# Second attention: where the queries' sums are added, and when the query parts, the one-hot products and the exponentials are issued

## The chip, the cores and the metric

The kernel runs on one core of one Trainium2 chip. The metric is the device time of one execution in microseconds, as the median over runs; lower is better. The profile of one further execution lists, for the same core, the busy time of every engine, the waits and the granted clock of TensorE.

## What is computed

The program is two layers, each a cross attention and a mixture of experts, on x of 4 x 256 x 512 in float32, with a context of 4 x 1601 x 512. The change lies in the second layer's attention alone:

```
def _L1_xattn_ref(text, features, Wq_w, Wq_b, Wk_w, Wk_b, fn_w, qn_w, kn_w):
    def rmsnorm(x, w):
        xf = x.astype(jnp.float32)
        var = jnp.mean(xf * xf, axis=-1, keepdims=True)
        return (xf * jax.lax.rsqrt(var + EPS)).astype(x.dtype) * w
    features_n = rmsnorm(features, fn_w)
    Q = jnp.einsum('btd,fd->btf', text, Wq_w) + Wq_b
    K = jnp.einsum('bsd,fd->bsf', features_n, Wk_w) + Wk_b
    Q = rmsnorm(Q, qn_w)
    K = rmsnorm(K, kn_w)
    scale = 1.0 / jnp.sqrt(jnp.asarray(K.shape[-1], dtype=Q.dtype))
    scores = jnp.einsum('btf,bsf->bts', Q, K) * scale
    attn = jax.nn.softmax(scores, axis=-1)
    attended = jnp.einsum('bts,bsf->btf', attn, features_n)
    return attended
x = x + _L1_xattn_ref(_layernorm(x, axis=-1), ctx_4096, ...)
```

## The kernel before

**Numbers in two parts.** Every large product is made of float32 operands split into a high part (rounded to the fast matmul format, made by ScalarE as a copy) and a low part (value minus high part, made by VectorE or GpSimd). TensorE then runs three matmuls for one product: high by high, high by low, low by high (the helper `three`, L1580 to L1582).

**Query part** (engine programs of `normed_attention_block`, before the loops). The 1024 rows of x are 8 tiles of 128; a batch i of 4 has two of them. For each batch TensorE transposes x (`transpose_x`, L1618), multiplies by the query weights in four column groups f (`project`, 12 matmuls of 256 columns each, into two halves of `ps_s` in turn), and one batch later multiplies the queries by the scaled key weights (`through_keys`, 4 x 12 matmuls). This way the keys are never projected: the scores are the queries, taken through the key weights, times the normalised context. ScalarE makes the high part of the queries (`qt_hi`, L1862) and their squares (L1864); VectorE makes the low part (`qt_lo`, L2012). `project` of group f waits for `qt_done` of group f - 2, since they share a half of `ps_s`. What the RMS norm of Q and the key bias need per query row are two sums over 512 features: of the squares, and of the query times `z_col` (norm weights times key bias). `query_sums` (L1643 to L1662) makes them as matmuls of one column in plain float32: per tile 4 for the squares (L1655), and 8 for the other sum (L1658 and L1660). The trace shows each plain float32 matmul as two instructions.

**Loop.** One iteration is one batch b, with 13 tiles of 128 context rows (the last has 65).

- Tile steps: ScalarE scales a tile (`scale_tile`), TensorE transposes it (L1668), ScalarE and VectorE split it into `k_hi` and `k_lo` (L1830, L1966), TensorE multiplies it by the Gram matrix of the key weights (`key_products`), VectorE adds a row (L2034) and sums it against the tile (L2036, two operands in SBUF) to get the norm of each key. ScalarE and GpSimd split the tile itself into `f_hi` and `f_lo` (L1895, L1566). At t = 1 ScalarE also writes `q_hi` of the batch (L1897), and at t = 2 GpSimd writes `q_lo` (L1574).
- Key norms: they lie one per partition and are needed along the columns. `turn_norms` transposes them, ScalarE takes the root, VectorE inverts (`invert`, L2047), and `spread_inverses` (L1723) multiplies with a one-hot matrix, so that every partition holds the row. These matmuls have 8 or 5 rows. ScalarE copies the result (`key_inverses`, L1884).
- Scores: `scores(j, ch)` for two query tiles j and four column chunks ch. VectorE scales them and takes the maximum (`scale_scores`, `largest`), ScalarE takes the exponential in two halves (`exponents`, L1910).
- Weighing: in eight steps (j, g) TensorE transposes the weights (`transpose_probs`, L1763), ScalarE and VectorE split them (`probs_hi` L1924, `probs_lo` L2069), and `weigh` multiplies by the context tiles. `output` (L2076 on) adds the result to x.

Each engine runs its own list in the order in which it is written, with semaphore waits between the engines; nothing reorders it. In the list of TensorE before, the lines that matter here stand so:

```
                    key_products(t)
                    if t == FIRST + 1:
                        turn_norms(0)
                spread_inverses(0)
...
                scores(0, 1)
                scores(0, 0).then_inc(s_ps, 1)
                scores(0, 2)
                turn_norms(1)
                scores(0, 3).then_inc(s_ps, 1)
                spread_inverses(1)
```

## Time and profile before

| What | Value |
|---|---|
| median of 3 runs | 3189.24 us (3187.05 to 3197.71) |
| profiled execution, its own time | 3184.14 us |
| its span, first to last instruction | 3182.4 us |
| TensorE matmul busy (PE) | 3049.8 us, 96% of the span |
| VectorE busy (DVE) | 2046.9 us, 64% |
| ScalarE busy (ACT) | 1727.0 us, 54% |
| GpSimd busy (POOL) | 871.5 us, 27% |
| mean granted clock of TensorE | 0.979 of full speed |

PE counts a matmul as busy from start to a modelled end, so it is also busy when it runs at half clock. "PEclk" in a table of stretches is the granted clock as a share of full speed (1 is 2.4 GHz, 0.5 is 1.2 GHz), averaged over the stretch; so stretch x (1 - PEclk) is the time that the lower clock cost in it, as long as TensorE had work. A row of the timeline gives start, length, engine, line, operation, and in brackets the idle time before it and what ended it.

### The profile page before, as it was taken

How to read it: one execution, taken by the hardware profiler on the slowest of the kernel's cores; microseconds unless marked ns; L12 is line 12 of the kernel's file. 1: busy time of each engine (PE TensorE's matmuls, PEld its weight loads, DVE VectorE, ACT ScalarE, POOL GpSimd, SP SyncE). 2: the span in 40 equal slices, each digit the busy share in tenths (PEclk: the TensorE clock that was granted, in tenths of full speed). 3: DMA queues.
4: the chain of work that ended last, by engine and by line, in shares of the span. 5: the costliest groups of instructions: out<-in, count | busy, mean ns of one | idle time of the engine just before them, and what ended most of it. 6: DMA issues, size and time to landing. Idle time of an engine off the chain costs nothing. (4 is left out here: it accounts for less than half of the span.)

```text
span 3182.4 us, 53416 instructions
## 1 busy us (share of the span) xinstructions
PE 3049.8 (96%) x18474; PEld 2704.4 (85%) x18474; DVE 2046.9 (64%) x3205; ACT 1727.0 (54%) x3218; POOL 871.5 (27%) x709
## 2 busy tenths in 40 slices
PE   8999998999999999999999999979979899998898
PEld 8888887899999999899998999978858897776786
DVE  4433333788888888788887888864464546554676
ACT  4433344667766666666666666642243334443473
POOL 0000121344444444444443444432200122221202
PEclk9999999999999999999999999999989989999999
DMA  7665696767777676677766777557631110111685
GB/s 251 217 215 197 206 289 201 151 159 163 163 159 163 159 159 161 155 158 158 162 159 156 158 161 161 129 143 240 203 133 77 34 36 29 41 41 40 213 290 163
DMA packets 376184, 497.59 MB, mean 156 GB/s; under 512 B 34348, under 2 KB 283484, under 8 KB 375928
## 3 DMA queue, kind: packets, MB, share of 16 engines
q1 hardware_dynamic: 373368, 485.93, 56.5%
q0 software_dynamic: 2560, 8.39, 0.8%
q8 instruction: 143, 2.34, 0.3%
q14 instruction: 113, 0.93, 0.1%
HBM read 226.09 MB, written 133.87 MB: 113 GB/s over the span
## 5 line engine op out<-in xcount | busy, mean ns | idle before, releaser
L725 POOL TENSOR_TENSOR a_t_lo<-a_turned,a_t_hi 128x512 fp32r<-128x512 f32 x512 | 649.7, 1290 | 938.5 <-ACT a_t_hi L854 938.5
L845 ACT ACTIVATE a_probs<-a_ps_s,a_neg_max 128x1024 f32<-128x1024 f32 (+1 forms) x512 | 529.5, 1034 | 474.4 <-DVE a_neg_max L897 468.7
L890 DVE TENSOR_REDUCE a_half_max<-a_ps_s 128x1 f32<-128x1024 f32 (+1 forms) x512 | 571.2, 1116 | 190.9 <-PE a_ps_s L742 186.8
L740 PE MATMUL a_ps_s<-a_k_buf,a_q_buf 128*128 128x512 f32 (+1 forms) x1024 | 419.6, 410 | 17.8 <-ACT a_probs L845 11.7
L741 PE MATMUL a_ps_s<-a_k_buf,a_q_buf 128*128 128x512 f32 (+1 forms) x1024 | 386.0, 377 | 0.0
L742 PE MATMUL a_ps_s<-a_k_buf,a_q_buf 128*128 128x512 f32 (+1 forms) x1024 | 385.1, 376 | 0.0
L926 DVE TENSOR_TENSOR a_x_lo<-a_ps_x,a_x_hi 128x512 fp32r<-128x512 f32 (+1 forms) x512 | 314.4, 614 | 107.1 <-ACT a_x_hi L863 107.1
L916 DVE STREAM_TRANSPOSE a_turned<-xn 128x512 f32<-128x512 f32 x512 | 357.7, 699 | 0.0
L472 DVE TENSOR_TENSOR p_out<-p_ps_j,p_out 128x512 fp32r<-128x512 f32 (+3 forms) x196 | 152.9, 780 | 303.8 <-ACT p_out L400 303.8
L400 ACT ACTIVATE p_out<-p_ps_j 128x512 fp32r<-128x512 f32 (+3 forms) x196 | 142.1, 725 | 312.0 <-PE p_ps_j L293 312.0
L740 PE MATMUL a_ps_o<-a_t_hi,a_v_buf 128*128 128x256 f32 x1024 | 298.9, 292 | 6.1 <-issue 3.6
L854 ACT ACTIVATE a_t_hi<-a_turned 128x512 fp32r<-128x512 f32 x512 | 298.5, 629 | 2.3 <-DVE a_turned L916 2.3
L863 ACT ACTIVATE a_x_hi<-a_ps_x 128x512 fp32r<-128x512 f32 (+1 forms) x512 | 274.5, 537 | 24.5 <-PE a_ps_x L770 12.8
L741 PE MATMUL a_ps_o<-a_t_lo,a_v_buf 128*128 128x256 f32 x1024 | 287.5, 281 | 0.0
L742 PE MATMUL a_ps_o<-a_t_hi,a_v_buf 128*128 128x256 f32 x1024 | 287.3, 281 | 0.0
L770 PE MATMUL a_ps_x<-a_turn,a_probs 128*128 128x128 f32 (+1 forms) x1792 | 279.1, 272 | 0.0
L740 PE MATMUL a_ps_o<-a_x_hi,a_v_buf 128*128 128x256 f32 (+1 forms) x896 | 262.4, 293 | 0.0
L742 PE MATMUL a_ps_o<-a_x_hi,a_v_buf 128*128 128x256 f32 (+1 forms) x896 | 251.8, 281 | 0.0
L741 PE MATMUL a_ps_o<-a_x_lo,a_v_buf 128*128 128x256 f32 (+1 forms) x896 | 251.4, 281 | 0.0
L770 PEld LDWEIGHTS a_ps_x<-a_turn,a_probs 128*128 128x128 f32 (+1 forms) x1792 | 219.0, 140 | 34.8 <-issue 0.2
L740 PEld LDWEIGHTS a_ps_s<-a_k_buf,a_q_buf 128*128 128x128 f32 x1024 | 194.9, 190 | 48.6 <-issue 11.7
L742 PEld LDWEIGHTS a_ps_s<-a_k_buf,a_q_buf 128*128 128x128 f32 x1024 | 194.6, 190 | 34.3
(437 smaller groups left out, 6944.6 us busy)
## 6 DMA issues: line engine op xcount, KB each, us to landing
xn<-a_probs SPq DMA_DIRECT2D x1024, 128.0 KB, 3.4
a_q_all<-p_out SPq DMA_DIRECT2D x64, 512.0 KB
a_q_buf<-a_q_all SPq DMA_DIRECT2D x128, 256.0 KB, 3.1
a_k_buf<-a_k_all SPq DMA_DIRECT2D x64, 464.5 KB, 4.0
a_v_all<-p_out SPq DMA_DIRECT2D x56, 512.0 KB
a_k_all<-p_out SPq DMA_DIRECT2D x48, 384.0 KB
a_v_buf<-a_v_all SPq DMA_DIRECT2D x64, 256.0 KB
a_o_all<-a_o_part SPq DMA_DIRECT2D x128, 128.0 KB, 3.1
```

The lines of the kernel that those rows point to most:

```text
L472: dve.tensor_tensor(job_views(n, 1)[0], ps, hi.bitcast(F32), ALU.subtract).then_inc(job_done, 1)
L725: pool.tensor_tensor(t_lo[:, slot, :, :], turned[:, slot, :, :], t_hi[:, slot, :, :].bitcast(F32), ALU.subtract).then_inc(t_done, 1)
L740: pe.matmul(o, w_hi, m_hi, start=first, stop=False)
L741: pe.matmul(o, w_hi, m_lo, start=False, stop=False)
L742: return pe.matmul(o, w_lo, m_hi, start=False, stop=last)
L770: tr = pe.transpose(ps_x[0:rows, bank, col:col + P], probs[j][u.a][:, c0:c0 + rows], turn[:, :])
L845: act.activation(probs[j][u.a][:, lo:hi], s_flat[:, lo:hi], ACT.Exp, bias=neg_max[:, j:j + 1], scale=SCALE, accum_out=half_sum[:, bass.ds( ...
L854: act.activation(t_hi[:, slot, :, :], turned[:, slot, :, :], ACT.Copy).then_inc(t_hi_done, 1)
L863: act.activation(x_hi[0:rows, slot, 0:m, :], ps_x[0:rows, bank, 0:TOK * m].rearrange("p (m n) -> p m n", m=m), ACT.Copy).then_inc(x_hi_don ...
L890: dve.reduce_max(half_max[:, half:half + 1], s_flat[:, lo:hi], AX.X).then_inc(max_done, 1)
L916: dve.transpose(turned[:, slot, :, :].rearrange("p k (q r) -> p k q r", r=SQ), traded[:, u.a, :, :, 2 * SQ * p:2 * SQ * (p + 1)].rearrange ...
L926: dve.tensor_tensor(x_lo[0:rows, slot, 0:m, :], ps_x[0:rows, bank, 0:TOK * m].rearrange("p (m n) -> p m n", m=m), x_hi[0:rows, slot, 0:m, ...
```

## The change

1. `query_sums` no longer sums over the four feature groups on TensorE. ScalarE writes a third tile per group, `biased_q` = (query + bias) x `z_col` (with a new column `z_bias`). GpSimd adds the four groups of the squares and of `biased_q` to one, each with an addition of 2 x 256 columns and one of 256, and TensorE makes one matmul of one column per sum and tile. VectorE's `qt_lo` now waits for the third tile (`q_read`) instead of the second.
2. The split of the scaled key weights (`w2_hi`, `w2_lo`) moves from the first batch of queries to a place ahead of the split of the query weights.
3. `q_hi` and `q_lo` of a batch are made during the weighing of the batch before (ahead of the loop for the first one), and `q_lo` by VectorE instead of GpSimd.
4. `spread_inverses(0)` moves behind `scores(0, 0)`.
5. The two exponentials of the second query tile move ahead of `probs_hi(0, 2)` and `probs_hi(0, 3)`.

```diff
@@ gpsimd
             pool.memset(k_lo[:, :, CTX:WIDTH].bitcast(F32), 0.0).then_inc(set_up, 1)
+            for i in range(B):
+                pool.wait_ge(q_read, DC * (i + 1))
+                for n, parts in enumerate((squared[i % 2], biased_q[i % 2])):
+                    pool.tensor_tensor(parts[:, 0:2, :], parts[:, 0:2, :], parts[:, 2:4, :], ALU.add).then_inc(q_added, 1)
+                    pool.wait_ge(q_added, 4 * i + 2 * n + 1)
+                    pool.tensor_tensor(parts[:, 0, :], parts[:, 0, :], parts[:, 1, :], ALU.add).then_inc(q_added, 1)
             pool.wait_ge(table_done, 3)
...
-                    if t == 2:
-                        pool.wait_ge(q_hi_done, b + 1)
-                        pool.tensor_tensor(q_lo[:, :, :].rearrange("p c n -> p (c n)"), queries[:, bass.ds(b, 1), :].rearrange("p a n -> p (a n)"),
-                                           q_hi[:, :, :].rearrange("p c n -> p (c n)").bitcast(F32), ALU.subtract).then_inc(q_done, 1)
@@ tensor
             def query_sums(i):
-                pe.wait_ge(q_squared, DC * (i + 1))
+                pe.wait_ge(q_added, 4 * (i + 1))
...
                 for j in range(QT):
                     at = QT * i + j
-                    for f in range(DC):
-                        pe.matmul(ps_p[:, 0, at:at + 1], squared[i % 2][:, f, j * P:(j + 1) * P], ones[:, 0:1],
-                                  start=f == 0, stop=f == DC - 1)
-                    for f in range(DC):
-                        pe.matmul(ps_p[:, 1, at:at + 1], qt_hi[i % 2][:, f, j * P:(j + 1) * P].bitcast(F32), z_col[:, f:f + 1],
-                                  start=f == 0, stop=False)
-                        mm = pe.matmul(ps_p[:, 1, at:at + 1], qt_lo[i % 2][:, f, j * P:(j + 1) * P].bitcast(F32), z_col[:, f:f + 1],
-                                       start=False, stop=f == DC - 1)
+                    pe.matmul(ps_p[:, 0, at:at + 1], squared[i % 2][:, 0, j * P:(j + 1) * P], ones[:, 0:1], start=True, stop=True)
+                    mm = pe.matmul(ps_p[:, 1, at:at + 1], biased_q[i % 2][:, 0, j * P:(j + 1) * P], ones[:, 0:1], start=True, stop=True)
                 mm.then_inc(qs_ps, 1)
...
-                spread_inverses(0)
...
                 scores(0, 0).then_inc(s_ps, 1)
+                spread_inverses(0)
                 scores(0, 2)
@@ scalar
                 normalize(t)
+            act.wait_ge(qk_w_done, 1)
+            for f in range(DC):
+                act.activation(w2_hi[:, f, :], key_w[:, f, :], ACT.Copy, scale=qk_w[:, f:f + 1]).then_inc(w2_hi_done, 1)
             weights_hi(0)
...
-                if i == 0:
-                    for f in range(DC):
-                        act.activation(w2_hi[:, f, :], key_w[:, f, :], ACT.Copy, scale=qk_w[:, f:f + 1]).then_inc(w2_hi_done, 1)
...
+                    act.activation(biased_q[i % 2][:, f, :], ps_s[:, f % 2, 0:TOK], ACT.Identity, scale=z_col[:, f:f + 1], bias=z_bias[:, f:f + 1]
+                                   ).then_inc(q_read, 1)
...
+            act.wait_ge(q_kept, DC)
+            query_hi(0)
             with act.Fori(0, B) as b:
...
-                    if t == 1:
-                        act.activation(q_hi[:, :, :].rearrange("p c n -> p (c n)"), queries[:, bass.ds(b, 1), :].rearrange("p a n -> p (a n)"),
-                                       ACT.Copy).then_inc(q_hi_done, 1)
...
-                exponents(0)
+                exponents(0, 0)
+                exponents(0, 1)
                 probs_hi(0, 0)
                 probs_hi(0, 1)
                 scale_tile(b + 1, 0)
                 scale_tile(b + 1, 1)
+                exponents(1, 0)
                 probs_hi(0, 2)
+                exponents(1, 1)
                 probs_hi(0, 3)
-                exponents(1)
 
                 act.activation(table_seed[:, :], eps_col[:, :], ACT.Sqrt)
+                query_hi((b + 1) % B)
@@ vector
+            dve.tensor_tensor(z_bias[:, :], z_col[:, :], columns[:, BQ, :], ALU.mult).then_inc(z_done, 1)
+            for f in range(DC):
+                dve.wait_ge(w2_hi_done, f + 1)
+                dve.scalar_tensor_tensor(w2_lo[:, f, :], key_w[:, f, :], qk_w[:, f:f + 1], w2_hi[:, f, :].bitcast(F32),
+                                         ALU.mult, ALU.subtract).then_inc(w2_done, 1)
             weights_lo(0)
...
-                    dve.wait_ge(q_squared, DC * i + f + 1)
+                    dve.wait_ge(q_read, DC * i + f + 1)
...
+            query_lo(0, 1)
             with dve.Fori(0, B) as b:
...
                 probs_lo(1, 1)
+                query_lo((b + 1) % B, b + 2)
                 output(0)
```

**Sums of a batch, on TensorE.** The end of `through_keys(0)` (L1582) and the start of `query_sums(0)`, before; the pair of `z_col` rows stands four times per tile, and the whole twice:

```order
L1582 MATMUL c_ps_s<-c_k_hi,c_f_lo 128x256
L1655 MATMUL c_ps_p<-ones,c_shared 128x1 x4
L1658 MATMUL c_ps_p<-c_z_col,c_k_hi 128x1
L1660 MATMUL c_ps_p<-c_z_col,c_k_lo 128x1
L1658 MATMUL c_ps_p<-c_z_col,c_k_hi 128x1
```

The same place in the change, with the transposes of x and the next product behind it (the names in `c_shared` are the added squares and the added `biased_q`; line numbers are those of the changed kernel):

```order
L1585 MATMUL c_ps_s<-c_k_hi,c_f_lo 128x256
L1656 MATMUL c_ps_p<-ones,c_shared 128x1
L1657 MATMUL c_ps_p<-ones,c_shared 128x1
L1656 MATMUL c_ps_p<-ones,c_shared 128x1
L1657 MATMUL c_ps_p<-ones,c_shared 128x1
L1621 MATMUL c_ps_t<-ident,xn 128x128 x8
L1583 MATMUL c_ps_s<-c_k_hi,c_f_hi 128x256
```

Of 24 matmuls of one column per batch 4 are left.

**One-hot products, on TensorE.** The end of the last key product, `spread_inverses(0)` and the start of the scores, before:

```order
L1581 MATMUL c_ps_s<-c_g_lo,c_k_hi 65x128
L1582 MATMUL c_ps_s<-c_g_hi,c_k_lo 65x128
L1723 MATMUL c_ps_p<-c_key_row,key_w 128x128 x8
L1778 REGISTER_ALU
L1580 MATMUL c_ps_s<-c_k_hi,c_q_hi 128x512
```

The same products in the change, between the last matmuls of `scores(0, 0)` and the first of `scores(0, 2)`:

```order
L1583 MATMUL c_ps_s<-c_k_hi,c_q_hi 128x512
L1584 MATMUL c_ps_s<-c_k_lo,c_q_hi 128x512
L1585 MATMUL c_ps_s<-c_k_hi,c_q_lo 128x512
L1719 MATMUL c_ps_p<-c_key_row,key_w 128x128 x8
L1583 MATMUL c_ps_s<-c_k_hi,c_q_hi 128x512
```

They moved behind 24 matmuls of 512 columns.

**Exponentials, on ScalarE.** From the scaling of the next batch's second tile (`c_raw`) to the switch back to the table of the root, before:

```order
L1824 ACTIVATE c_raw<-c_raw,c_inverse 128x512
L1917 REGISTER_ALU
L1923 ISA
L1924 ACTIVATE c_t_hi<-c_ps_t 128x512
L1917 REGISTER_ALU
L1923 REGISTER_ALU
L1924 ACTIVATE c_t_hi<-c_ps_t 65x128
L1910 ACTIVATE c_shared,c_half_sum<-c_shared,c_neg_max,c_q_now 128x1024
L1910 ACTIVATE c_shared,c_half_sum<-c_shared,c_neg_max,c_q_now 128x577
L1936 ACT_TABLE_LOAD
```

And in the change:

```order
L1820 ACTIVATE c_raw<-c_raw,c_inverse 128x512
L1912 ACTIVATE c_shared,c_half_sum<-c_shared,c_neg_max,c_q_now 128x1024
L1919 REGISTER_ALU
L1925 ISA
L1926 ACTIVATE c_t_hi<-c_ps_t 128x512
L1912 ACTIVATE c_shared,c_half_sum<-c_shared,c_neg_max,c_q_now 128x577
L1919 REGISTER_ALU
L1925 REGISTER_ALU
L1926 ACTIVATE c_t_hi<-c_ps_t 65x128
L1940 ACT_TABLE_LOAD
```

Each half of the second tile's exponential now stands ahead of one of the two copies `c_t_hi` that it followed.

## Rows read from the trace of the kernel before

**Rows 1.** Busy time by stretch: queries, then the four iterations; count, PEclk, DMA share, GB/s.

```profile
2501.00:2585.30 84.30, 82.36 (x599) 81.59 (x598) 22.22 (x45) 20.26 (x44) 0.00 (x0) 0.85 0.01 3
2585.30:2669.70 84.40, 80.55 (x437) 68.95 (x438) 45.59 (x82) 36.88 (x66) 20.80 (x15) 0.93 0.13 40
2669.70:2754.40 84.70, 78.81 (x437) 66.87 (x436) 49.01 (x82) 36.73 (x66) 20.27 (x15) 0.96 0.13 39
2754.40:2837.60 83.20, 77.29 (x438) 65.64 (x437) 48.99 (x82) 36.80 (x66) 20.33 (x15) 0.98 0.11 39
2837.60:2922.40 84.80, 78.89 (x437) 66.61 (x435) 49.02 (x82) 36.77 (x66) 20.34 (x15) 0.96 0.13 39
```

**Rows 2.** Waits of PE, 2501 to 2922 us: total, times, longest.

```profile
PE c_ps_s L1580 <- DVE c_k_lo L1966: 7.6, 13, 1.4
PE c_ps_t L1763 <- ACT c_shared L1910: 6.6, 4, 1.7
PE c_ps_p L1723 <- DVE c_key_row L2047: 6.3, 8, 1.4
PE c_ps_s L1580 <- DVE c_k_lo L2012: 1.9, 2, 1.6
```

**Rows 3.** Busy time by stretch: first and last `query_sums`, and what follows.

```profile
2521.60:2528.10 6.50, 6.50 (x51) 6.50 (x49) 0.42 (x1) 0.00 (x0) 0.00 (x0) 0.81 0.00 0
...
2577.60:2585.30 7.70, 7.70 (x50) 7.70 (x49) 0.42 (x1) 0.00 (x0) 0.00 (x0) 0.67 0.00 0
2585.30:2590.30 5.00, 5.00 (x21) 4.71 (x22) 1.75 (x6) 2.65 (x5) 1.44 (x2) 0.50 0.00 0
```

**Rows 4.** Timeline of PE: start and slowing of the first `query_sums`.

```profile
2521.61 0.95 PE L1655 MATMUL c_ps_p<-ones,c_shared 128*128 128x1 f32 x8
...
2525.54 0.54 PE L1658 MATMUL c_ps_p<-c_z_col,c_k_hi 128*128 128x1 f32 x2
```

**Rows 5.** Timeline: a query group in the third batch, from ScalarE to TensorE's next-but-one group.

```profile
2532.60 0.48 ACT L1862 ACTIVATE c_k_hi<-c_ps_s,c_columns 128x256 fp32r<-128x256 f32 x1 [1.94 <-PE c_ps_s L1582]
2532.97 0.47 ACT L1864 ACTIVATE c_shared<-c_ps_s,c_columns 128x256 f32<-128x256 f32 x1
...
2534.01 0.38 PE L1580 MATMUL c_ps_s<-c_k_hi,c_f_hi 128*128 128x256 f32 x1
```

**Rows 6.** Line L1554, GpSimd: an elementwise operation of 512 columns (ns min/median/max).

```profile
L1554 POOL TENSOR_TENSOR c_f_lo<-key_w,c_f_hi x4: 1283/1288/1295, 2480.4 to 2484.1; 128x512 fp32r<-128x512 f32 x4
```

**Rows 7.** Timeline of ScalarE: the last tile of squares of the last batch.

```profile
2557.80 0.47 ACT L1864 ACTIVATE c_shared<-c_ps_s,c_columns 128x256 f32<-128x256 f32 x1
```

**Rows 8.** Timeline, tile steps of the second iteration: GpSimd's `q_lo` and what follows.

```profile
2678.57 2.39 POOL L1574 TENSOR_TENSOR c_q_lo<-xn,c_q_hi 128x1024 fp32r<-128x1024 f32 x1
2678.71 2.79 DVE L2036 SCALAR_TENSOR_TENSOR c_shared<-c_shared,c_raw 128x512 f32<-128x512 f32 x1
...
2682.17 0.50 PE L1580 MATMUL c_ps_s<-c_g_hi,c_k_hi 128*128 128x512 f32 x1 [1.44 <-DVE c_k_lo L1966]
...
2682.74 1.69 DVE L2036 SCALAR_TENSOR_TENSOR c_shared<-c_shared,c_raw 128x512 f32<-128x512 f32 x1
```

**Rows 9.** Line L2036, VectorE, all iterations (ns min/median/max); timeline of VectorE, a later tile step.

```profile
L2036 DVE SCALAR_TENSOR_TENSOR c_shared<-c_shared,c_raw x52: 686/693/2795, 2590.6 to 2872.7; 128x512 f32<-128x512 f32 x48, 65x512 f32<-65x512 f32 x4
...
2689.58 0.69 DVE L2034 TENSOR_TENSOR c_shared<-c_ps_s,c_u_row 128x512 f32<-128x512 f32 x1 [0.29 <-PE c_ps_s L1582]
```

**Rows 10.** Second iteration: `spread_inverses(0)` in PE's timeline, and the stretch of scores behind it.

```profile
2704.24 2.05 PE L1723 MATMUL c_ps_p<-c_key_row,key_w 8*128 8x128 f32 x16 [1.41 <-DVE c_key_row L2047]
...
2706.20:2711.80 5.60, 5.60 (x18) 4.48 (x18) 0.00 (x0) 0.60 (x1) 0.00 (x0) 0.70 0.84 240
```

**Rows 11.** Timeline, second iteration: maximum of the second tile, and its exponential.

```profile
2733.24 0.27 DVE L2061 TENSOR_SCALAR c_neg_max<-c_half_max,c_q_now 128x1 f32<-128x1 f32 x1
...
2737.95 1.23 ACT L1910 ACTIVATE c_shared<-c_shared,c_neg_max,c_q_now 128x1024 f32<-128x1024 f32 x1
```

**Rows 12.** Line L1032, VectorE: an operation of the shape of `q_lo` (ns min/median/max).

```profile
L1032 DVE TENSOR_TENSOR y_o_lo<-y_o_scaled,y_o_hi x32: 1211/1218/2291, 2127.9 to 2299.5; 128x1024 fp32r<-128x1024 f32 x32
```

More of the change, by code:

```diff
@@ L1456, in normed_attention_block @@
         columns = sb("columns", [P, 5, DC])
-        qk_w, z_col = sb("qk_w", [P, DC]), sb("z_col", [P, DC])
+        qk_w, z_col, z_bias = sb("qk_w", [P, DC]), sb("z_col", [P, DC]), sb("z_bias", [P, DC])
         bk_square, eps_col, table_seed = sb("bk_square", [P, 1]), sb("eps_col", [P, 1]), sb("table_seed", [P, 1])
@@ L1471, in normed_attention_block @@
         squared = [shared[:, a * DC * TOK:(a + 1) * DC * TOK].rearrange("p (c n) -> p c n", c=DC) for a in range(2)]
+        biased_q = [at.rearrange("p (c n) -> p c n", c=DC) for at in (shared[:, 2 * DC * TOK:3 * DC * TOK], key_inv[:, D:D + DC * TOK])]
         bk_wide = key_inv[:, 0:DC * P].rearrange("p (c n) -> p c n", c=DC)
@@ L1498, in normed_attention_block @@
         xt_ps, xt_hi_done, xt_done = sem("xt_ps"), sem("xt_hi_done"), sem("xt_done")
-        qp_ps, qt_hi_done, q_squared, qt_done, qk_ps, q_kept, qs_ps, root_done, q_recip, table_done = (sem(n) for n in (
-            "qp_ps", "qt_hi_done", "q_squared", "qt_done", "qk_ps", "q_kept", "qs_ps", "root_done", "q_recip", "table_done"))
+        qp_ps, qt_hi_done, q_squared, q_read, q_added, qt_done, qk_ps, q_kept, qs_ps, root_done, q_recip, table_done = (sem(n) for n in (
+            "qp_ps", "qt_hi_done", "q_squared", "q_read", "q_added", "qt_done", "qk_ps", "q_kept", "qs_ps", "root_done", "q_recip", "table_done"))
         c_root, c_inv, f_scaled, f_hi_done, f_done = (sem(n) for n in ("c_root", "c_inv", "f_scaled", "f_hi_done", "f_done"))
@@ L1646, in query_sums @@
             def query_sums(i):
-                pe.wait_ge(q_squared, DC * (i + 1))
+                pe.wait_ge(q_added, 4 * (i + 1))
                 if i == 0:
-                    pe.wait_ge(z_done, 1)
                     pe.wait_ge(u_done, 1)
@@ L1850, in _ @@
             inputs_hi(0)
-            act.wait_ge(qk_w_done, 1)
+            act.wait_ge(z_done, 2)
             for i in range(B):
@@ L1873, in _, with query_hi @@
             act.wait_ge(qk_ps, DC * B)
+            def query_hi(place):
+                act.activation(q_hi[:, :, :].rearrange("p c n -> p (c n)"), queries[:, bass.ds(place, 1), :].rearrange("p a n -> p (a n)"),
+                               ACT.Copy).then_inc(q_hi_done, 1)
+            act.wait_ge(q_kept, DC)
+            query_hi(0)
             with act.Fori(0, B) as b:
@@ L1905, in _, with exponents @@
                 key_inverses(3)
-                def exponents(j):
+                def exponents(j, half):
+                    lo, hi = HALVES[half]
                     act.wait_ge(neg_max_done, QT * b + j + 1)
-                    for half, (lo, hi) in enumerate(HALVES):
-                        act.activation(probs[j][:, lo:hi], probs[j][:, lo:hi], ACT.Exp, bias=neg_max[:, j:j + 1], scale=q_now[:, SC, j:j + 1],
-                                       accum_out=half_sum[:, j, half:half + 1]).then_inc(probs_done, 1)
+                    act.activation(probs[j][:, lo:hi], probs[j][:, lo:hi], ACT.Exp, bias=neg_max[:, j:j + 1], scale=q_now[:, SC, j:j + 1],
+                                   accum_out=half_sum[:, j, half:half + 1]).then_inc(probs_done, 1)
                 def probs_hi(j, g):
@@ L1986, in _ @@
             dve.tensor_tensor(z_col[:, :], qk_w[:, :], columns[:, BK, :], ALU.mult).then_inc(z_done, 1)
+            dve.wait_ge(z_done, 1)
+            dve.tensor_tensor(z_bias[:, :], z_col[:, :], columns[:, BQ, :], ALU.mult).then_inc(z_done, 1)
[3 more added lines that the diff above has]
+                                         ALU.mult, ALU.subtract).then_inc(w2_done, 1)
             weights_lo(0)
@@ L2004, in _ @@
                     inputs_lo(i + 1)
-                if i == 0:
-                    for f in range(DC):
-                        dve.wait_ge(w2_hi_done, f + 1)
-                        dve.scalar_tensor_tensor(w2_lo[:, f, :], key_w[:, f, :], qk_w[:, f:f + 1], w2_hi[:, f, :].bitcast(F32),
-                                                 ALU.mult, ALU.subtract).then_inc(w2_done, 1)
                 for f in range(DC):
-                    dve.wait_ge(q_squared, DC * i + f + 1)
+                    dve.wait_ge(q_read, DC * i + f + 1)
                     dve.scalar_tensor_tensor(qt_lo[i % 2][:, f, :], ps_s[:, f % 2, 0:TOK], columns[:, BQ, f:f + 1],
@@ L2029, in _, with query_lo @@
             dve.wait_ge(sums_set, 1)
+            def query_lo(place, count):
+                dve.wait_ge(q_hi_done, count)
+                dve.tensor_tensor(q_lo[:, :, :].rearrange("p c n -> p (c n)"), queries[:, bass.ds(place, 1), :].rearrange("p a n -> p (a n)"),
+                                  q_hi[:, :, :].rearrange("p c n -> p (c n)").bitcast(F32), ALU.subtract).then_inc(q_done, 1)
+            query_lo(0, 1)
             with dve.Fori(0, B) as b:
```

## The prediction

> **What bounds the kernel now.** I read the busy times by stretch first, over the part of the program that the change touches: the queries (84.3 us) and the four iterations of the loop [rows 1]. In all five TensorE is busy for 93 to 98% of the stretch, and no other engine for more than 58%. So TensorE's own list sets the time here, and a microsecond counts if it shortens that list, removes a wait in it, or lets it run at the higher clock. The same rows give the granted clock: 0.85 in the queries, 0.93 to 0.98 in the loop. The lower of its two levels (1.2 instead of 2.4 GHz) cost 84.3 x 0.15 = 12.6 us in the queries, and 84.4 x 0.07 + 84.7 x 0.04 + 83.2 x 0.02 + 84.8 x 0.04 = 14.4 us in the loop.
>
> Then the list of TensorE's waits: 7.6 us for `k_lo`, 6.6 us for the exponentials, 6.3 us for the inverted key norms, 1.9 us for the queries' low parts, 22.4 us together [rows 2]. Last the timeline around these places, to see what the engine that was waited for did before.
>
> **The change, part by part.** The sum is made against the profiled execution, 3184.1 us; that is 5.1 us below the median shown.
>
> *Sums of the queries, work.* The first `query_sums` takes 6.5 us at a clock of 0.81, so 5.3 us at full clock, the last 7.7 x 0.67 = 5.2 [rows 3]. Four of them are some 20.9 us. What is left per batch is 4 matmuls, 8 instructions in the trace; eight such take 0.95 us [rows 4], four batches 3.8. Difference: **-17.1 us**.
>
> *Sums of the queries, clock.* The first `query_sums` starts with eight instructions in 0.95 us; 3.9 us later two of them take 0.54 us [rows 4], the clock has fallen. The last is followed by 5.0 us at a clock of 0.50, already in the first iteration [rows 3]. So one-column matmuls are what the engine did before these falls, and a new stretch of them is as short as the part that still ran at full clock. I take it that the clock no longer falls: **-12.6 us** in the queries and 5.0 x 0.5 = **-2.5** at the start of the loop. The other bound is nothing.
>
> *A third tile on ScalarE, and a later low part.* In the third batch ScalarE starts the two tiles of a group 0.37 us apart, VectorE follows, and TensorE's next-but-one group starts 1.41 us after the first of them [rows 5]. The third tile adds a step. Its nearest bounds are that spacing, 0.37, and a tile's full length, 0.48; it has a scale and a bias by partition, so I take 0.45. It delays one group per batch, since the group after that finds its half of PSUM ready: 4 x 0.45 = **+1.8**. ScalarE is busy for 20 of the 84 us [rows 1]; 16 tiles more, 7 us, do not make it the bound.
>
> *The split of the key weights, moved.* Of the 1.9 us of waits in the queries, 1.6 are one wait in the first batch, behind the two engines' work on the key weights [rows 2]; 0.3 would be there as in later batches: **-1.3**. At the new place VectorE's four operations of 512 columns could delay TensorE's transposes of the weights by nothing, or by all of their 4 x 0.69 = 2.8 us, at the length of L2036 [rows 9]. I take 0: VectorE has nothing to do there until TensorE has transposed the first weights. The Trainium skill (page "SBUF — State Buffer", section "Who interferes with whom") speaks against it: a VectorE instruction with two SBUF inputs waits for the whole of a GpSimd instruction that reads SBUF, and GpSimd normalises two tiles of x at that time. By that rule VectorE would be late, and with 0.8 us (an estimate) of it on TensorE the sum would be -53.8 instead of -54.6. The long L2036 beside GpSimd's `q_lo`, 2.79 us [rows 8], agrees with that rule.
>
> *Additions on GpSimd.* Per batch two of 512 columns at 1.29 us [rows 6] and two of 256; these no row shows, so between half of that, 0.65, and all, 1.29. Together 3.9 to 5.2 us. They start when ScalarE is done with a batch. In the last batch that is at 2558.3 us [rows 7], and its sums start at 2577.6 [rows 3]: 19.3 us, of which the sums of the batch before (6 to 8 us) and the lower clock take some 10 away. About 9 us cover 5.2: cost 0. Uncovered it would be 4 x 3.9 = 15.6 us.
>
> *Query parts, in the loop.* While GpSimd writes `q_lo` for 2.39 us, VectorE's L2036, started 0.14 us later, takes 2.79 us instead of its median of 0.69 and ends after it; the next one takes 1.69, and TensorE waits 1.44 us [rows 8, 9]. `q_lo` is made in every iteration, and I count three with this wait: 3 x 1.44 = 4.3 us. The second slow L2036 is 1.0 us late, against 0.3 us that VectorE idles per step [rows 9]; I put 0.3 us on TensorE for it, 0.9 in all. These are **-5.2** of the 7.6 us for `k_lo` [rows 2]. At the new places ScalarE spends at most 1.23 us per batch (an operation of its 1024 columns [rows 11]) and VectorE 1.22 us [rows 12], during the weighing. If both were on the path, that would be 4 x 2.45 = 9.8 us; VectorE idles there and elsewhere for 35 of 84 us [rows 1], ScalarE for more, and TensorE is two steps ahead with its transposes: 0. Ahead of the loop they follow the sums at once; between 0 and 2.45, I take **+0.5**, since TensorE has a key product to do at that point.
>
> *One-hot products behind the scores.* Four waits of 1.4 us for the inverted norms, 5.6 of the 6.3 us [rows 2], go: **-5.6**. Late next would be VectorE's scaling of the scores, which needs the spread norms; but it needs `scores(0, 0)` as well, and it then inverts the second part of the norms in time for the second one-hot product, for which I leave the 0.7 us of waits as they are.
>
> *Exponentials.* The maximum of the second tile is ready at 2733.5 us, but its exponential starts at 2737.95, since it stands behind two copies that wait for TensorE [rows 11]. Ahead of them it ends some 3 us earlier than now, and TensorE's wait, at most 1.7 us, goes four times: **-6.6** [rows 2].
>
> *Clock in the loop.* Without the first 2.5 us, 11.9 of the 14.4 us remain. In the second iteration the scores behind `spread_inverses(0)` run at 0.70; before that the engine had waited 1.41 us and run one-hot matmuls of 8 rows for 2.05 us [rows 10]. The wait goes, the 2 us stay. No row shows one without the other: the bounds are nothing and -11.9, and I take the middle, **-6.0**.
>
> Sum: -17.1 - 12.6 - 2.5 + 1.8 - 1.3 - 5.2 + 0.5 - 5.6 - 6.6 - 6.0 = **-54.6 us**, 3184.1 to 3129.5. Runs of the kernel before lie 3 to 14 us above its profiled one, so I forecast 3131.
>
> **Rivals.**
>
> *GpSimd late.* TensorE waits for `q_added` in each batch: the two additions of a sum depend on each other, and VectorE may hold GpSimd up. For it: TensorE's list is shorter and comes sooner. Against it: some 9 us of cover over 5.2. If nothing were covered, +15.6 us: 3147.
>
> *The clock stays low.* Short sums and one-hot products still bring it down in every batch and iteration. For it: small matmuls precede the falls in both places. Against it: the full clock at the start of rows 4. Then 12.6 + 2.5 + 6.0 come back: 3152.
>
> *The loop moves its waits.* The edits in the loop don't do what they say, because the chain of norms, maximum and exponential is as long as before and TensorE waits for it elsewhere. Against it: the three waits have three different releasers. If all of 5.6 + 6.6 + 5.2 comes back: 3148.
>
> *VectorE and GpSimd meet in every tile step.* This one ends slower. GpSimd's `f_lo`, of 512 columns, runs once per tile, as L2036 does; with the steps shifted, the two could meet in each of the 52. VectorE has 0.3 us to spare per step. At the 1.69 us of rows 8 each step costs 1.0 - 0.3 = 0.7, 36 us in all, 3167; at the 2.79 us, 1.8, 94 us, 3225. It decides the sign from 54.6 / 52 + 0.3 = 1.35 us of delay per step. Against it: the median of 52 is 0.69 [rows 9], and the edits leave the order within a step alone. The page named above has the rule for it: whichever of the two comes first holds the shared port for its whole instruction. By that rule one meeting costs at most one `f_lo`, 1.29 us here, just short of the deciding point.
>
> **How the numbers follow.** Forecast 0.82; GpSimd late 0.05; clock 0.05; waits moved 0.05; the meeting 0.03. A measurement of this kernel tells some 0.3%, 9.6 us, from no change. The first four are faster by more, 0.97, less 0.01 for two of them together with a meeting: 0.96. The rest is 0.02 within and 0.02 slower. The forecast's own range is 6 us down for the clock in the loop, as much up, and some 10 either way for the runs and the taken middles: 3115 to 3147. Reaching for the first and third rival, the upper end becomes 3150.
>
> **What would show it.** Right: a query stretch of about 54 us with a clock near 1.0; no wait of TensorE for GpSimd there; no L2036 above 2 us; no wait at `transpose_probs(1, 0)`; iterations of 77 to 79 us. Wrong: TensorE waiting for the added tiles; a clock of 0.85 in the queries; a new wait of over 1 us at the one-hot products or at `transpose_probs(0, 0)`; a median of L2036 above 1 us.

## The result, and the profile after

| | before | changed |
|---|---|---|
| median of the runs, us | 3189.06 (3187.05 to 3197.71, 4 runs) | 3138.94 (3133.83 to 3140.45, 4 runs) |
| ratio, with 95% interval | 1 | 0.9835 [0.9813, 0.9856] |
| span of the profiled execution, us | 3182.4 | 3135.9 |

The change makes the kernel 1.6% faster, some 50 us. The page of the changed kernel, its first lines:

```profile
span 3135.9 us, 53132 instructions
## 1 busy us (share of the span) xinstructions
PE 3018.5 (96%) x18314; PEld 2674.1 (85%) x18314; DVE 2043.5 (65%) x3211; ACT 1734.3 (55%) x3235; POOL 873.2 (28%) x721
```

The answer to [rows 1]: TensorE by stretch, the queries and then the four iterations. The columns are length, busy time, granted clock, DMA share, GB/s.

```profile
2505.70:2561.00 55.30, 52.65 (x438) 1.00 0.02 5
2561.07:2636.88 75.81, 75.31 (x430) 0.98 0.14 44
2638.01:2717.21 79.20, 78.20 (x438) 0.96 0.13 41
2717.21:2794.82 77.61, 76.61 (x437) 0.98 0.14 42
2794.82:2874.00 79.18, 78.18 (x437) 0.96 0.14 41
```

The queries take 55.3 us in place of 84.3, and the clock no longer falls in them. The iterations are 5 to 8 us shorter, but their clock is almost what it was.

The answer to [rows 2], TensorE's waits from 2490 to 2880 us:

```profile
PE c_ps_s L1583 <- DVE c_k_lo L2018: 2.6, 4, 1.2
PE c_ps_s L1583 <- DVE c_k_lo L1971: 1.8, 6, 0.4
...
PE c_ps_p L1719 <- DVE c_key_row L2060: 0.7, 4, 0.2
```

The wait for the exponentials is gone, the one for `key_row` is down from 6.3 to 0.7 us, the one for the keys' `k_lo` (L1971, before L1966) from 7.6 to 1.8. No row names GpSimd's additions. The one row that grew is the queries' low part (L2018, before L2012).

For all comparisons below I measure the same marks in each trace: from the transpose of the vectors, with which the second attention begins, to the first transpose of the second context tile ("queries"), and from there by iteration. The first iteration is counted to the transposes of the next batch's first tile, 1.1 us ahead of that mark, in every kernel alike. "Low" is the length of the stretches in the loop at a granted clock of 0.50, found by reading the clock every 0.85 us; each costs half its length, since the work takes twice as long there (the second and third iteration of before, with 6.8 and 3.4 us of it, take 84.7 and 83.1 us). Every such stretch in the loop lasted 3.4 or 6.8 us.

A trace is of one execution. The last two columns are of all: span x (1 - mean granted clock) is an estimate of what the lower clock cost in an execution, wherever in it. "Clock" is its mean minus that of the kernel before on the same chip (there 71.5 to 73.1 us), "rest" the same for what remains of the span; 4 to 10 executions against 9 to 25, standard errors 0.7 to 2.3 us.

| kernel | queries, us | iterations, us | low in the loop, us | clock, all executions, us | rest, all executions, us |
|---|---|---|---|---|---|
| before | 105.6 | 83.3, 84.7, 83.1, 84.8 | 5.1 + 23.8 | | |
| changed | 76.8 | 75.8, 79.2, 77.6, 79.2 | 20.4 | | |
| changed, again | 78.0 | 77.4, 79.2, 77.6, 79.2 | 23.8 | -13.3 | -39.4 |
| sums alone | 78.3 | 79.4, 84.7, 83.2, 84.7 | 20.4 | -18.7 | -14.9 |
| sums spread out | 95.4 | 79.4, 84.7, 84.7, 83.2 | 20.4 | -19.2 | +3.4 |
| one-hot alone | 108.5 | 83.7, 81.7, 81.8, 81.8 | 5.5 + 17.0 | -5.7 | -4.3 |
| exponentials alone | 108.7 | 81.4, 84.4, 82.8, 84.5 | 5.1 + 34.0 | +6.2 | -8.9 |
| query parts alone | 105.7 | 82.5, 82.4, 82.4, 84.0 | 5.1 + 30.6 | +2.1 | -9.3 |
| `q_lo` on VectorE, in place | 105.5 | 83.5, 84.7, 83.1, 81.6 | 5.6 + 27.2 | +1.9 | -4.6 |
| `q_lo` on GpSimd, early | 108.5 | 82.7, 82.5, 82.4, 82.4 | 5.5 + 27.2 | +1.8 | -8.2 |
| short chunk first | 77.5 | 77.8, 78.3, 76.7, 78.2 | 13.6 | -17.1 | -37.0 |
| one-hots between | 77.5 | 78.4, 80.2, 80.2, 80.2 | 0 | -25.7 | -21.3 |

(The first of two terms is what reaches from the queries into the loop.) One execution of the kernel with the additions made twice took 10322 us and is left out.

One thing in the column of the queries is not the edits'. Behind the 5 us in which TensorE has almost nothing to do as the second attention begins, there is a low stretch ahead of the first query product: of 3.4 us in the traces of before, changed, query parts alone and `q_lo` in place, and of 6.8 us in the other traces of the table, where it takes 22.6 to 22.9 us from the first mark to that product for 21.4 to 21.6.

From its first mark to the first transpose of the routed experts the second attention takes 449.2 us before and 396.3 us changed: -52.9, by -28.8 in the queries and -24.1 in the loop.

### The profile page after: what moved, and what is told of

Its sections match the earlier page's. It is cut to its first block and busy times, and to the rows that moved or that the text cites. A ratio compares the mean times of both kernels' runs of the same rounds, so it can differ in the third digit from the quotient of the medians.

```text
span 3135.9 us, 53132 instructions
## 1 busy us (share of the span) xinstructions
PE 3018.5 (96%) x18314; PEld 2674.1 (85%) x18314; DVE 2043.5 (65%) x3211; ACT 1734.3 (55%) x3235; POOL 873.2 (28%) x721
```

## The experiments

Each kernel is timed against the kernel before on the same chip; where the effect is a few microseconds, the table above tells more than the ratio.

**The sums alone.** Kernel of before with all edits to the query part, and none to the loop.

```
+            for i in range(B):
+                pool.wait_ge(q_read, DC * (i + 1))
+                for n, parts in enumerate((squared[i % 2], biased_q[i % 2])):
...
-                pe.wait_ge(q_squared, DC * (i + 1))
+                pe.wait_ge(q_added, 4 * (i + 1))
```

> Kernel of before with the query part of the change alone (GpSimd's additions, ScalarE's third tile, split of the key weights moved); the loop as before. The prediction's theory: sums' work -17.1, clock of the query part -12.6, clock at the loop's start -2.5, third tile +1.8, split moved -1.3, together about -31.7 us, and the query stretch at a granted clock near 1.0 and some 55 us long in place of 84.3; the loop's iterations stay at 84.4, 84.7 and 83.2 us. Rival 1, the clock falls for another reason than the one-column matmuls: about -17 us, stretch still near .85. Rival 2, most of the gain needs the loop's parts: under -10 us.

Measured: 3156.43 against 3190.07 us, ratio 0.9893 [0.9877, 0.9910], -33.6 us. The queries shrink by 27.4 us, the second to fourth iteration stay where they were, to 0.1 us. Queries and start of the loop:

```profile
2506.40:2563.31 56.91, 53.40 (x443) 1.00 0.04 11
2563.31:2642.67 79.36, 75.49 (x430) 0.98 0.14 42
2642.67:2727.40 84.73, 78.84 (x437) 0.96 0.13 39
```

The clock's part, 18.7 us less over all executions, comes with the query edits alone. So the sums and the loop are two separate gains.

**The sums spread out.** The 24 one-column matmuls per batch stay, one or two behind each triple of the product through the key weights.

```
                     for f in range(DC):
...
+                        at = DC * c + f
+                        for one in small[3 * at // 2:3 * (at + 1) // 2]:
+                            last = small_matmul(*one)
+                last.then_inc(qs_ps, 1)
```

> Kernel of before with the same 24 one-column matmuls per batch, but set one or two at a time between the triples of the product through the key weights, so that no stretch consists of them. If the place of the small matmuls lowers the clock (the prediction's theory): the clock's terms come alone, -12.6 and -2.5, so about -15 us, granted clock near 1.0 over the query stretch. Rival 1, the small matmuls lower the clock wherever they stand: about 0. Rival 2, a small matmul costs little between long ones, so their work of 17 us goes too: -25 us or more, near sums_alone, and the split into work and clock in the prediction was only a way of counting.

Measured: 3173.95 us, 0.9953 [0.9936, 0.9970], -16.1 us. From the first projections to the loop:

```profile
2500.20:2574.44 74.24, 70.92 (x603) 1.00 0.03 8
```

The same matmuls, and the clock stays up. It was their standing in a row that brought it down, and the clock's term of the sum exists by itself. Both kernels run these queries at full clock, so their difference, 95.44 - 78.27 = 17.2 us, is the work in this form, less what the third tile and the moved split of the key weights cost together, which only the kernel with the sums alone has (+0.5 by the forecast). Rival 2 is out: between long matmuls the short ones cost no less. By the rest of the span, 3.4 us longer over all executions, they cost a little more.

**One-hot products alone.**

```
-                spread_inverses(0)
...
                 scores(0, 0).then_inc(s_ps, 1)
+                spread_inverses(0)
```

> Kernel of before with the first eight one-hot matmuls moved behind the scores of two chunks, nothing else. Theory: the wait for VectorE's reciprocals at key_row goes, 4 x 1.4 = -5.6 us, and with the one-hot stretch split from the wait the clock gives back up to 6 us more, -5.6 to -12 us. Rival 1: the wait comes back at another place (maximum, exponentials), about 0. Rival 2, suggested by the trace of the changed kernel: the falls of the clock move from the first one-hot group to the second, so that the waits' 5.6 us come and nothing of the clock.

Measured: 3181.38 us, 0.9968 [0.9954, 0.9982], -8.7 us. The wait falls to 0.7 us. With half the low time taken off, the later iterations go from 81.4 (84.73 - 3.4) to 80.0 us. Four of the five falls in the loop now stand behind the second one-hot group, where before it was one of five: they moved, as the second rival had it, but the low time shrank too. In the profiled execution the first low stretch of the one-column sums lasted 10.2 us where it had lasted 6.8, and the one ahead of the queries 6.8 for 3.4, in code that is the same: the 3 us more in that column are not the edit's. Nor is the 1.6 us for which TensorE waits for `k_lo` in the first iteration: there GpSimd's `q_lo` met VectorE as it does in the other iterations (9.1 us of that wait in all, for 7.6).

**Exponentials alone.**

```
-                probs_hi(0, 2)
-                probs_hi(0, 3)
-                exponents(1)
+                exponents(1, 0)
+                probs_hi(0, 2)
+                exponents(1, 1)
+                probs_hi(0, 3)
```

> Kernel of before with the two exponentials of the second query tile each ahead of a copy of the first tile's probabilities, nothing else. Theory: the wait at the second tile's first transposition goes, 4 x 1.65 = -6.6 us. Rival: the copies pushed behind the exponentials make TensorE wait for the third and fourth transposed group instead, 4 x 1.2 us, so about -2 us or 0.

Measured: 3186.71 us, 0.9991 [0.9981, 1.0000]: -3.4 us, and no change is not excluded. Among TensorE's waits the exponentials no longer appear, and nothing takes their place:

```profile
PE c_ps_s L1580 <- DVE c_k_lo L1968: 7.5, 13, 1.4
...
PE c_ps_p L1723 <- DVE c_key_row L2049: 6.2, 8, 1.4
```

Yet the second to fourth iteration are only 0.3 us shorter each. The clock took the rest back. Three iterations, and the stretch behind the one-hot products of the first of them:

```profile
2673.79:2758.22 84.43, 80.26 (x437) 0.94 0.12 39
2758.22:2841.05 82.83, 78.64 (x437) 0.96 0.13 40
2841.05:2925.53 84.48, 80.30 (x437) 0.94 0.12 39
2709.50:2710.50 1.00, 1.00 (x7) 0.82 0.00 0
2710.50:2716.50 6.00, 6.00 (x19) 0.50 0.65 210
2716.50:2717.50 1.00, 1.00 (x5) 0.77 0.75 287
```

The low stretch there lasts some 6.8 us; before it lasted 3.4 in that iteration. In the loop the low time grows from 23.8 to 34.0 us, which costs 5.1 of the 6.6 us. This trace is of the longest of ten executions, but the ten together say the same: the clock costs 6.2 us more than before, the rest 8.9 us less. My rival had the right size and the wrong reason: the copies do not make TensorE wait.

**Query parts alone, and two variants.** The split of a batch's queries is made in the weighing of the batch before; in the first variant only the engine changes, in the second only the place. The expectations follow in this order.

The edit of the first, ScalarE and VectorE:

```
-                    if t == 1:
-                        act.activation(q_hi[:, :, :].rearrange("p c n -> p (c n)"), queries[:, bass.ds(b, 1), :].rearrange("p a n -> p (a n)"),
...
                 act.activation(table_seed[:, :], eps_col[:, :], ACT.Sqrt)
+                query_hi((b + 1) % B)
...
                 probs_lo(1, 1)
+                query_lo((b + 1) % B, b + 2)
```

of the second, GpSimd and VectorE:

```
-                        pool.wait_ge(q_hi_done, b + 1)
...
+                    if t == 2:
+                        dve.wait_ge(q_hi_done, b + 1)
```

and of the third, where `query_lo` is GpSimd's, behind its last `f_lo` of the iteration:

```
+                query_lo((b + 1) % B, b + 2)
```

> Kernel of before with the query parts alone: both halves of the split made during the weighing of the batch before, the rest of it on VectorE. Prediction's theory: the waits for the remainders of the keys early in each iteration go, -5.2 us, +0.5 ahead of the loop, and VectorE does not meet GpSimd (no operation of L2036 over 2 us). Rival, from exps_alone: a removed wait of the loop is partly given back by longer low stretches of the clock, so anything from -5 to 0 us while the waits themselves are gone.

> Kernel of before, only the subtraction for q_lo moved from GpSimd to VectorE, in the same place (third tile step). If the meeting of the two engines makes the long operation (the prediction's theory): the 2.8 us operation shrinks to 1.5 and VectorE pays 1.2 us for the subtraction itself, so the wait of TensorE changes little, -1 to +2 us in all, and the gain of the change came from the place as much as from the engine. Rival: the place is indifferent and the engine is all, -5 us.

> As parts_alone, but the subtraction stays on GpSimd, in the weighing. If only the place counts: the same waits go as in parts_alone, -5 us before the clock's share. If the two engines meet wherever they run together: an operation of VectorE in the weighing (remainders of the probabilities, 0.69 us; the output's update) becomes longer by up to 1.2 us, and TensorE waits up to that long for c_t_lo in each of four iterations, so that 0 to 5 us of the gain are lost.

Measured: 0.9977 [0.9968, 0.9987], 0.9992 [0.9981, 1.0003] and 0.9974 [0.9963, 0.9985]; -6.3, -3.7 and -6.6 us. TensorE's wait for the keys' `k_lo` falls from 7.6 us to 1.8, 3.7 and 1.8. With half the low time taken off, the later iterations take 79.0, 79.7 and 79.0 us for 81.4. So the place is enough, on either engine, and the engine alone gives some 70% of it in these traces and half of it over all executions (rest -4.6 for -9.3). My theory for the first variant was almost nothing, since VectorE pays: its total does not exclude that, but the wait and the iterations speak against it. For the second variant VectorE and GpSimd do meet in the weighing, but at an operation that nobody waits for. Timeline of VectorE, then of GpSimd:

```profile
2668.26 0.69 DVE L2078 TENSOR_TENSOR c_t_lo<-c_ps_t,c_t_hi 128x512 fp32r<-128x512 f32 x1 [5.15 <-ACT c_t_hi L1932]
2668.86 1.11 DVE L2115 TENSOR_TENSOR c_row_sum<-c_half_sum 128x2 f32<-128x2 f32 x1
...
2667.58 2.38 POOL L1565 TENSOR_TENSOR c_q_lo<-xn,c_q_hi 128x1024 fp32r<-128x1024 f32 x1 [40.08 <-ACT c_q_hi L1880]
```

`t_lo`, whose first input is in PSUM, keeps its 0.69 us. The sum of two columns, both inputs in SBUF, takes 1.11 us and ends with GpSimd's instruction, at 2669.97 and 2669.96.

**Additions twice.** The changed kernel, with each addition of GpSimd made once more into unused memory.

```
+                    pool.tensor_tensor(f_lo[:, 12, :].rearrange("p (a n) -> p a n", a=2), parts[:, 0:2, :], parts[:, 2:4, :], ALU.add).then_inc(q_twice, 1)
+                    pool.wait_ge(q_twice, 4 * i + 2 * n + 1)
+                    pool.tensor_tensor(f_lo[:, 12, 0:TOK], parts[:, 0, :], parts[:, 1, :], ALU.add).then_inc(q_twice, 1)
```

> The changed kernel with GpSimd's additions of each batch made twice (once into unused memory, then as they are), 4.1 us more of GpSimd per batch. The prediction counts 0 for the additions because 9 us of product lie over 4.1 us of them: by that doubling costs 0 to 1 us against the changed kernel. Rival 1, the cover is shorter than counted: up to 4 x 4.1 = 16 us. Rival 2, GpSimd's additions lengthen VectorE's operations beside them, as the 1.02 us for a copy of 0.62 us suggests: 0.4 to 1 us per batch, 2 to 4 us.

> As adds_twice, for its trace: TensorE's wait for c_k_lo in the batches shows whether 4.1 us more of GpSimd lengthen VectorE's operations (waits 2.6 us before, up to 5 us then), and a wait for GpSimd at the one-column matmuls whether the cover was used up.

Measured: 0.9837 [0.9818, 0.9856] and 0.9821 [0.9800, 0.9843]: like the changed kernel's own 0.9835. The trace of the second has the end of the last batch's additions and its sums:

```profile
2553.72 0.73 POOL L1573 TENSOR_TENSOR c_key_inv<-c_key_inv 128x256 f32<-128x256 f32 x1
...
2557.08 0.28 PE L1662 MATMUL c_ps_p<-ones,c_shared 128*128 128x1 f32 x2
```

2.6 us are left between the last addition, which ends at 2554.45, and the sums, with twice the work. The queries' waits for `k_lo` are 2.6 us in all, as before doubling. The cover is not used up, and more additions lengthen nothing that counts.

**The short chunk first.** Run beside the changed kernel itself. The short fourth chunk's scores move ahead, so that the second one-hot group no longer follows a row of short matmuls.

```
+                scores(0, 3)
                 scores(0, 1)
                 scores(0, 0).then_inc(s_ps, 1)
                 spread_inverses(0)
-                scores(0, 2)
-                turn_norms(1)
-                scores(0, 3).then_inc(s_ps, 1)
+                scores(0, 2, turn=True).then_inc(s_ps, 1)
                 spread_inverses(1)
```

> The changed kernel once more, beside the next one and on the same chip: about 3139 us, 20 us of low clock in the loop in six stretches of 3.4 us, none in the query part.

> The changed kernel with the scores of the short fourth chunk (66 columns) moved ahead of the other chunks of the first tile, the second norm transposition into the third chunk's scores, VectorE's second reciprocal ahead of the maximum, and the copy for the one-hot table ahead of the batches. If the fall behind the second one-hot group comes from the row of short matmuls there (short chunk, transposition, one-hots, 3.0 us in a row): four falls go, 4 x 1.7 = -6.8 us, and the copy gives -0.7, about -7.5 us against the changed kernel. Rival 1, the falls come behind the one-hots wherever the short chunk stands: 0 to -1 us. Rival 2, the chain of VectorE from the first scores to the exponentials becomes late by the short chunk's 1.3 us: up to +5 us.

Measured: 3137.97 us, 0.9834 [0.9819, 0.9848], for the changed kernel and 3137.80, 0.9833 [0.9816, 0.9849], for this one: the same. Low time is 13.6 us in place of 20.4 or 23.8, but the second one-hot group now waits up to 0.7 us:

```profile
PE c_ps_p L1719 <- DVE c_key_row L2061: 2.7, 4, 0.7
```

The reason was at most half right: of the four falls behind the second one-hot group three remain. And of the 3.4 to 5.1 us that the clock gave in the traces, half of the low time that went, the longer wait took 2.0 again.

**One-hots between the scores.** To end both the row and the wait: each one-hot by itself behind a part of the scores, and the second norms turned early.

```
-                spread_inverses(0)
...
+                        if c < len(between):
+                            spread_inverse(between[c])
```

> The changed kernel with every one-hot matmul by itself behind one chunk's share of the scores of a 128-column part (12 triples' columns between two of them), the short fourth chunk first, the second norm transposition in a transposition bank so that its root and reciprocal are early, and the one-hot table copied ahead of the batches. If rows of short matmuls bring the low stretches of the loop: the six or seven of 3.4 us go, 10 to 12 us gained, the copy 0.7, no wait at key_row, so 8 to 13 us under the changed kernel, iterations of 75 to 76 us. Rival 1, one-hots lower the clock also one at a time: 0 to -1 us. Rival 2, the falls only move to the short chunk: -1 to -5 us.

Measured: 3140.95 us, 0.9853 [0.9840, 0.9867]: no gain over the changed kernel, by the iterations a loss of 1 to 3 us in each. But the clock does what the theory said:

```profile
2558.88:2637.30 78.42, 78.05 (x430) 1.00 0.14 43
2637.30:2717.51 80.21, 79.37 (x437) 1.00 0.13 41
2717.51:2797.75 80.24, 79.41 (x438) 1.00 0.13 41
2797.75:2877.95 80.20, 79.36 (x437) 1.00 0.13 41
```

No low stretch is left. The loss is in the one-hots. Timeline of TensorE in this kernel:

```profile
2672.59 0.48 PE L1721 MATMUL c_ps_p<-c_key_row,key_w 8*128 8x128 f32 x2
2673.01 0.50 PE L1583 MATMUL c_ps_s<-c_k_hi,c_q_hi 128*128 128x512 f32 x1
...
2673.90 0.48 PE L1721 MATMUL c_ps_p<-c_key_row,key_w 8*128 8x128 f32 x2
```

and in the changed kernel, at the start of a group of eight:

```profile
2673.62 0.40 PE L1583 MATMUL c_ps_s<-c_k_hi,c_q_hi 128*128 128x512 f32 x1
...
2674.42 2.05 PE L1719 MATMUL c_ps_p<-c_key_row,key_w 8*128 8x128 f32 x16
2676.40 0.50 PE L1583 MATMUL c_ps_s<-c_k_hi,c_q_hi 128*128 128x512 f32 x1
```

With a one-hot between them the triples follow one another at 1.31 us, without at 0.70: 0.61 us for one that stands alone. In the group, eight take 2676.40 - 2673.62 - 0.70 = 2.08 us, 0.26 each. Thirteen per iteration cost 13 x 0.35 = 4.6 us more; the iterations grew from 75.8 (79.2 - 3.4) to 80.2. The executions agree with that: against the changed kernel (again) the clock costs 12.4 us less, the rest 18.1 us more. The row of these short matmuls costs clock, breaking it up into single ones costs more. Groups of two to four were not tried.

## Why the prediction was right, and where it was not

The forecast was 3131 us in a range of 3115 to 3150; 3138.94 lies within it, 8 us above the forecast. The sign was right, and so was the mechanism in every step but one, the clock in the loop. Step by step:

*The base.* The sum was made from 3184.1 us, an execution 5.1 us below the median, and I added only 1.5 us to come back to the runs. From the median it would have been 3189.1 - 54.6 = 3134.5. So 3.5 of the 8 us lie here, and 4.5 in a gain of 50.1 us in place of 54.6. What that execution had less of was low clock: 3182.4 x (1 - 0.979) = 67 us of it (an estimate as in the table), where the means beside the experiments are 71.5 to 73.1. How loosely one profile stands for the runs shows before the second attention even starts: in 13 profiles, with the same code up to there, it began between 2479.0 and 2486.8 us. For before and changed it was 2479.7 and 2484.3, which is most of why the spans differ by 46.5 us where the second attention itself gained 52.9; another 1.8 us lie behind it.

*Sums' work, third tile, split of the key weights* (-17.1 + 1.8 - 1.3 = -16.6). The queries of before without the clock's loss, 105.6 - 12.6 = 93.0, became 76.8 in the changed kernel: -16.2. (The 78.3 of the kernel with the sums alone have 1.5 us from the longer low stretch ahead of them; over all executions its rest fell by 14.9 us, with a standard error of 1.7.) The third tile is as estimated, 0.47 us of wait in three of the batches. In the second batch the wait is 1.2 us, which I had not seen coming: VectorE's copy of the one-hot table, 8 x 1024, ran into GpSimd's first addition. VectorE, then GpSimd:

```profile
2514.59 1.02 DVE L2025 COPY key_w<-ident 8x1024 f32<-8x1024 f32 x1
...
2513.77 1.29 POOL L1565 TENSOR_TENSOR c_shared<-c_shared 128x512 f32<-128x512 f32 x1 [18.50 <-ACT c_shared L1862]
2515.14 1.06 POOL L1567 TENSOR_TENSOR c_shared<-c_shared 128x256 f32<-128x256 f32 x1
```

The copy takes 1.02 us here and 0.62 before, GpSimd's second addition 1.06 where it takes 0.73 to 0.74 in the other batches. The rule that I had cited against another edit says that the first comer holds the shared port for its whole instruction (the Trainium skill, page "SBUF — State Buffer", section "Who interferes with whom"); both lengths agree with it, to 0.07 and 0.14 us: with a wait for the other's end they would be 1.09 and 1.20 us. At the key weights, where I had weighed that rule's 0.8 us, it cost nothing: the first low part of the query weights starts 12.86 us after the first mark, before 12.81. And there the trace differs from the rule. VectorE's four operations on the key weights, then their lengths (shortest, median, longest, ns), then GpSimd's second normalisation of x:

```profile
2493.33 3.08 DVE L1996 SCALAR_TENSOR_TENSOR c_f_lo<-key_w,c_qk_w,c_f_hi 128x512 fp32r<-128x512 f32 x4 [0.98 <-ACT c_f_hi L1839]
L1996 DVE SCALAR_TENSOR_TENSOR c_f_lo<-key_w,c_qk_w,c_f_hi x4: 740/740/1095, 2493.3 to 2495.7; 128x512 fp32r<-128x512 f32 x4
2493.12 2.06 POOL L1558 TENSOR_SCALAR xn<-x_res,c_mean_var,c_x_inverse 128x512 f32<-128x512 f32 x1
```

VectorE comes second, with both inputs in SBUF, and one of its operations takes 1.09 us instead of 0.74. Had the first waited until GpSimd's end at 2495.18, the four would have ended at some 2497.9; they ended at 2496.41. So not every such meeting costs the whole of the other's instruction; what made this one cheap is open.

*Sums' clock* (-12.6 and -2.5). Right: clock 1.00, from the first query product on, in both kernels that end the row of one-column matmuls, by fewer of them or by spreading them.

*Additions on GpSimd* (0). Right, with more cover than the 9 us that I counted: with the additions doubled, which take 8.6 us, 2.6 us were left.

*Query parts, one-hot products, exponentials* (-5.2 + 0.5 - 5.6 - 6.6). All three waits went as named. At full clock the single edits are worth 2.4, 1.4 and 2.0 us per later iteration, together 5.8; the whole change gives 81.4 - 75.8 = 5.6. They add up, and they are worth more than the rows of the waits say, 17.4 / 4 = 4.35. The timeline of before shows one reason. Transposes and key product of two tile steps:

```profile
2677.78 0.63 PE L1668 MATMUL c_ps_t<-ident,c_raw 128*128 128x128 f32 x4
2678.17 0.48 PE L1580 MATMUL c_ps_s<-c_g_hi,c_k_hi 128*128 128x512 f32 x1
...
2680.11 0.62 PE L1668 MATMUL c_ps_t<-ident,c_raw 128*128 128x128 f32 x4
```

The product that does not wait starts 0.39 us after the transposes; the one that waits 1.44 us starts at 2682.17 [rows 8], 2.06 us after them. A wait of 1.44 us costs 1.67: TensorE also loses the overlap of the two instructions. (The one-hot edit shows no such surplus: 1.4 us of wait, 1.4 us gained.)

*Clock in the loop* (-6.0). This step failed. I had put the fall down to wait and one-hot products together and taken the middle. Without the wait the low time is 20.4 or 23.8 us, 23.8 before: -1.7 us or nothing. With the sums alone, whose loop still waits, it is 20.4 us too. Over all executions the clock costs 18.7 us less than before with the sums alone, and 13.3 us less with the loop's edits as well: by that the loop's edits cost 5 us of clock (standard error 2; part of it may lie behind the loop), where I had them give 6. Of the six falls in the trace of the changed kernel four stand behind the second one-hot group, where before three of four iterations had none. So the short matmuls bring the clock down without the wait, and with the row broken up (one-hots between) no fall is left. That the total came out is luck in this part, since two errors nearly met: in the traces the loop gave 24.1 us where the sum had -25.4, by 2.5 at its start as forecast, 1.7 of clock in place of 6.0, and 19.9 in place of 16.9 for waits. Over all executions of the changed kernel (again) the clock, queries and loop together, gave 13.3 us where the sum had 21.1, and the rest 39.4 where it had 33.5.

*The rivals.* GpSimd late: no wait for it. The clock stays low: wrong for the queries, true for the loop. The loop moves its waits: no wait came back, but the clock can take its place, as the exponentials alone show. VectorE and GpSimd in every step: the median of the key sums stayed at 0.69 us, their longest fell from 2.80 to 1.47.

## What to carry to other kernels

Short matmuls in a row have two prices, their work and the clock of what follows; spread the row once, unchanged in number, and the two are measured apart. Before you break a row up for good, price one short matmul standing alone: here the clock's 10 us (20.4 / 2) cost 18 (4 x 4.6). And make a sum against the median of the runs, with the differences between profiles taken stage by stage, not span against span.

## What I had not expected of the hardware

The clock fell while TensorE was busy without a gap. In the changed kernel, around the first one-hot group of the second iteration (2674.42 to 2676.47, no wait ahead of it):

```profile
2673.62:2677.07 3.45, 3.45 (x23) 1.00 0.81 271
2677.07:2680.49 3.42, 3.42 (x10) 0.50 0.39 148
```

In the queries and the loop of these traces the low stretches lasted 3.4, 6.8 or 10.2 us, and in the trace with 1.65 us of wait taken away (exponentials alone) two of the four behind the first one-hot group were twice as long as before. What decides between one length and the next is open.

A one-hot matmul of 128 columns costs 0.26 us in a row of its kind and 0.61 us between matmuls of 512. Whether its weights, its 8 rows or the other type of its operands is the reason was not tried.

VectorE's sum of two columns, 0.15 us otherwise, took 1.11 us beside GpSimd and ended with it: what this meeting cost was set by what GpSimd still had to do, not by the size of VectorE's own operation. The operations on the key weights show that not every meeting goes so.
